# Start-up merged into the attention loop, and the feed-forward as one unrolled block with other engines for its maxima

## The reference, cut to what matters

```
h = tok(x)            # x 16x256x128: 5-step windows -> linear 640->256, +b, relu, batch norm with running mean, var
h = h + attn(layernorm(h))   # 252 rows per sequence, 16 heads of 16, bias by distance (32 buckets), causal softmax, Wo, +bo
h = h + ffn(layernorm(h))

def ffn(x):           # act_qdq: scale = max|x| over the WHOLE tensor / 32767, round, times scale
    x    = act_qdq(x)
    up   = act_qdq(x @ dq4(w_up).T)              # dq4: 4-bit weights, one scale per 32
    gate = act_qdq(x @ dq4(w_gate).T)
    gate = act_qdq(gate * round16(sigmoid(gate)))
    o    = act_qdq(gate * up)
    return o @ dq4(w_down).T
```

## Time and profile before

| what | us |
|---|---|
| three runs, median (lowest to highest) | 849.69 (849.53 to 849.99) |
| the profiled execution | 851.06 |
| its span, first to last instruction | 849.2 |
| busy: PE, DVE, ACT, POOL | 621.2, 619.2, 430.2, 182.2 |
| mean granted clock of PE, as a share of full speed | 0.893 |

### The profile page before, as it was taken

The page is one execution under the profiler, slowest core; times in us unless marked ns, Lnnn a source line. Parts: engine busy times, 40 slices in busy tenths (PEclk is TensorE's granted clock), DMA queues, the critical chain, the costliest instruction groups (busy, mean ns, idle before and its releaser), DMA issues. The chain is left out here.

```text
span 849.2 us, 15260 instructions
## 1 busy us (share of the span) xinstructions
PE 621.2 (73%) x5130; PEld 464.5 (55%) x5130; DVE 619.2 (73%) x965; ACT 430.2 (51%) x622; POOL 182.2 (21%) x228
## 2 busy tenths in 40 slices
PE   2625789898999988998989886299997720002998
PEld 1224577777777777777777654144443310002998
DVE  5656777898888888888988763346579996995442
ACT  0501434664446654466544553144498872444772
POOL 1121221122211222212222000000036552550000
PEclk9976999999999999999999975599999975555999
DMA  6233022221333312333122200000033312661343
GB/s 178 89 124 44 11 35 46 57 47 29 50 44 56 54 29 41 47 53 56 32 38 51 39 13 13 13 0 0 0 147 154 158 53 73 218 220 49 113 133 97
DMA packets 40063, 57.37 MB, mean 68 GB/s; under 512 B 5820, under 2 KB 31868, under 8 KB 40028
## 3 DMA queue, kind: packets, MB, share of 16 engines
q1 hardware_dynamic: 38876, 56.13, 26.2%
q10 hardware_dynamic: 1152, 0.79, 0.4%
HBM read 25.06 MB, written 19.13 MB: 52 GB/s over the span
## 5 line engine op out<-in xcount | busy, mean ns | idle before, releaser
L724 DVE TENSOR_REDUCE mx<-ps 126x2 f32<-126x504 f32 (+1 forms) x192 | 124.6, 674 | 44.4 <-PE ps L585 44.0
L1376 PE MATMUL ps<-wdT,oh 128*126 128x256 f16 x384 | 66.2, 280 | 92.7 <-DVE ol L1336 92.7
L807 ACT ACTIVATE pt<-sbr 126x504 f32<-126x504 f32 x192 | 114.8, 617 | 26.1 <-DVE sbr L715 24.9
L715 DVE TENSOR_TENSOR sbr<-ps,biasT 126x504 f32<-126x504 f32 x192 | 120.0, 675 | 8.9 <-PE ps L603 8.4
L1376 PEld LDWEIGHTS ps<-wdT,oh 128*126 128x126 f16 x384 | 48.9, 140 | 93.5 <-DVE ol L1336 93.5
L582 PE MATMUL ps<-biasN,identb 126*126 126x504 bf16 x192 | 75.8, 395 | 25.6 <-DMA k_st<-kl 25.6
L880 POOL TENSOR_TENSOR h<-h,bc 126x512 f32<-126x512 f32 x16 | 20.2, 1266 | 291.0 <-ACT h L821 291.0
L585 PE MATMUL ps<-k_st,q_st 65*126 65x252 f16 (+1 forms) x512 | 76.2, 252 | 0.0
L1047 PE MATMUL ps<-x2t,wgT 128*128 (+1 forms) x288 | 63.7, 386 | 11.0 <-DVE x2t L1090 11.0
L1047 PE MATMUL ps<-x2t,wuT 128*128 (+1 forms) x288 | 63.4, 376 | 11.1 <-ACT raw L1216 11.0
L585 PEld LDWEIGHTS ps<-k_st,q_st 65*126 65x126 f16 x512 | 61.5, 142 | 16.2 <-issue 1.9
(11 more groups left out here) (174 smaller groups left out, 1428.7 us busy)
## 6 DMA issues: line engine op xcount, KB each, us to landing
up_raw<-raw SPq DMA_DIRECT2D x14, 756.0 KB, 3.2
raw<-up_raw SPq DMA_DIRECT2D x14, 756.0 KB, 4.4
q_st<-qh SPq DMA_DIRECT2D x32, 128.0 KB, 4.0
k_st<-kh SPq DMA_DIRECT2D x32, 128.0 KB, 4.0
res<-hall SPq DMA_DIRECT2D x16, 252.0 KB
hin<-res SPq DMA_DIRECT2D x16, 252.0 KB
out<-y SPq DMA_DIRECT2D x16, 252.0 KB
xin<-in_x SPq DMA_DIRECT2D x16, 128.0 KB, 3.6
```

Source lines behind the costliest of these rows:

```text
L715: nc.vector.tensor_tensor(sbr[0:TT, n % 4].rearrange("p (h w) -> p h w", w=w), ps[0:TT, score_bank[name, n], 0:2 * N].rearrange("p (h w) - ...
L724: nc.vector.tensor_reduce(mx[0:TT, 0 if w == TT else 1, heads[0]:heads[-1] + 1], ps[0:TT, score_bank[name, n], 0:2 * N].rearrange("p (h w) ...
L807: nc.scalar.activation(pt[0:TT, n // 3 % 2, n % 3], sbr[0:TT, n % 4], ACT.Exp).then_inc(S["exp_r"], 1)
L1376: last = nc.tensor.matmul(ps[0:TT, s, t * C:(t + 1) * C], o[par][:, m, rows], wdT[:, w, m], start=(m == 0 and i == 0), stop=(m == MT - 1 a ...
```

## The change

The two first blocks become one and the two last become one. `sp_first`, `pool_first`, `dve_first`, `act_first`, `pe_first` run ahead of step -2 and call step -3 in their middle; the tiles of the start-up lie in buffers of the attention that are not used yet. Identity and mirror image are loaded. The running variance is loaded as a row for every partition, and POOL takes its `pow` on 128x256 numbers. `biasN` stays reversed: the mirror image takes the place of the identity in the matmul that adds it to the scores. `biasT` is put in order in step -1. Attention weights are split one after the other, the last (Wo) in step -1.

Of the feed-forward weights only the gate's is loaded and prepared in the attention (steps -1 and 0); up and down are loaded at the start of the feed-forward and prepared by DVE, PE and ACT between the gate's units. All maxima over partitions become a PE transpose of a broadcast column and a DVE maximum over 128 columns.

The feed-forward has no loops. The first two units of the up product go ahead of the last two of the gate; `raw` has five buffers; five units are never written to DRAM; ACT, not POOL, rounds the up product; the first sequence pair of the down product is made in six pieces instead of two. The last piece of the diff is ACT's loop over the gate's units, where `take` copies an up unit to `raw`.

```
-                nc.gpsimd.tensor_tensor(var[:], var[:], nhalf[:], ALU.pow).then_inc(S["vec_ready"], 1)
...
+            pool.wait_ge(S["vec_in"], 96)
+            nc.gpsimd.tensor_scalar(vec[:, 1, :], vec[:, 1, :], EPS, 1.0, ALU.add, ALU.mult
...
+            nc.gpsimd.tensor_tensor(vec[:, 1, :], vec[:, 1, :], nhalf[:, 0:1].broadcast_to([128, C]), ALU.pow
...
+            sp.dma_start(cw_n, cw.rearrange("(o p) k -> p o k", p=128)).then_inc(S["cw_in"], 16)
+            load_x(sp, 0)
...
+            sp.dma_start(biasN[0:TT], bass.AP(line_n, 0, [[1, TT], [LINE, H], [1, N]])).then_inc(S["biasN_in"], 16)
+            sp.dma_start(flipT[0:TT], bass.AP(line_t, 0, [[1, TT], [LINE, H], [1, N]])).then_inc(S["bias_in"], 16)
+            sp.dma_start(ff_view(0), ff_dram[0]).then_inc(S["ff_in0"], 16)
...
-        FF_DVE = {(-2, ("u", 2)): [("ffabs", 0)], (-2, ("stats", 2)): [("ffdq", 0, 0)],
-                  (-2, ("xnl", 2)): [("ffdq", 0, 1)], (-1, ("kl", 1)): [("ffdq", 0, 2), ("ffpow", 0)]}
+        FF_DVE = {(-2, ("u", 2)): [("wlo", 0, 1)], (-2, ("stats", 2)): [("wlo", 0, 2)], (-1, P1[2]): [("wlo", 0, 3)],
+                  (-1, ("ql", 2)): [("ffabs", 0), ("ffdq", 0, 0)], (0, P2[1]): [("ffpow", 0)]}
+        for i, at in enumerate((P1[0], P1[1], P1[2], P1[3], P1[4], P1[5], P1[6], P1[7])):
+            FF_PE[-1, at] = [("flip", 0, i)]
...
+        def over_partitions(pe, name):
+            wait(pe, "ared", SPREAD.index(name) + 1)
+            nc.tensor.transpose(spread_at(name), col[name].broadcast_to([128, 128]), identf[:]).then_inc(S["par"], 1)
+        def gathered(dve, name):
+            wait(dve, "par", SPREAD.index(name) + 1)
+            small(dve, nc.vector.tensor_reduce(col["p" + name], spread_at(name), X, ALU.max))
...
+        SEQ = [("g", t) for t in range(TL - 2)] + [("u", 0), ("g", TL - 2), ("u", 1), ("g", TL - 1)]
+        SEQ += [("u", t) for t in range(2, TL)]
...
+                def up_and_down(c):
+                    if c == 0:
+                        ff_largest(dve, 1)
+                        ff_largest(dve, 2)
+                    elif c == 1:
+                        power(dve, 6, 8, 4, 7, 256)
...
+                        ff_integers(dve, 1)
+                    elif c == 2:
+                        ff_integers(dve, 2)
+                for c in range(CH - 1):
                     integers(c + 1)
+                    largest_gate(2 * c)
+                    up_and_down(c)
+                    if 0 <= 2 * c - 5 < len(late):
+                        late_low(2 * c - 5)
+                    largest_gate(2 * c + 1)
+                    if 0 <= 2 * c - 4 < len(late):
+                        late_low(2 * c - 4)
...
+                for t in range(TL):
+                    wait(act, "p_r", t - 2)
+                    nc.scalar.activation(gq[t % 3][:], gat[:, t], ACT.Copy, scale=col["inv_g"]
...
+                    nc.scalar.activation(sig[t % 2][:], gq[t % 3][:], ACT.Sigmoid, scale=col["size_g"]
+                    if t + 3 < TL:
+                        take(t + 3)
```

More of the change, by code:

```diff
@@ new lines, in square, with spread @@
+        def square(w, part, km, i):
+            cols = w[:, part, km // 2, km % 2 * 128:km % 2 * 128 + 128]
+            return cols.rearrange("p (r s) -> p r s", s=8) if i < 2 else cols
+        def spread(pe, first, end, bank, at):
+            pe.wait_ge(S["wamax"], end)
+            for i in range(first, end):
+                last = nc.tensor.transpose(ps[:, bank, at + (i - first) * 128:at + (i - first + 1) * 128],
+                                           wam[:, i:i + 1].broadcast_to([128, 128]), identf[:])
+            last.then_inc(S["wspread"], 1)
@@ new lines, in pe_first @@
+        def pe_first(pe):
+            pe.wait_ge(S["consts"], 32)
+            for i in range(2):
+                nc.tensor.matmul(ps[0:H, i, 0:LINE], rel_s, hot_s[:, i * LINE:(i + 1) * LINE],
+                                 start=True, stop=True).then_inc(S["lines_ps"], 1)
+            pe.wait_ge(S["ident"], 16)
+            pe.wait_ge(S["cw_in"], 16)
+            for j, group in enumerate(banks):
+                for n, g in enumerate(group):
+                    last = nc.tensor.transpose(ps[:, 2 + j, n * 128:(n + 1) * 128], g[0], identf[:])
+                last.then_inc(S["wT_ps"], 1)
+            pe_step(pe, -3, 1)
+            spread(pe, 0, 1, 4, 256)
+            spread(pe, 1, 5, 5, 0)
@@ L970, in _ @@
             def _(pool):
-                for b in range(-3, 2):
+                pool_first(pool)
+                for b in range(-2, 2):
                     pool_step(pool, b, b % 2)
@@ L1059, in audio_tower @@
[L1059 to L1074 removed]
+        RING, KEPT = 5, 5
@@ L1334, in low @@
+                def low(c):
+                    for i, (m, e) in enumerate(pieces_of(c)):
+                        wait(dve, "oh_r", pieces_before(c) + i + 1)
+                        if i == 0 and c >= 2:
                             for bb in range(2):
-                                wait(dve, f"dn_ps{2 * par + bb}", k)
-                        nc.vector.tensor_tensor(flat(ol[par], hf), flat(oq, hf), flat(oh[par], hf), ALU.subtract
-                                                ).then_inc(S["ol_r"], 1)
@@ L1381, in _ @@
-                from_zero(pe, CH // 2, body)
+                over_partitions(pe, "ax")
+                for kind, t in SEQ:
+                    if kind == "g":
+                        wait(pe, "xq_r", t // 2 + 1)
+                    elif t == 0:
+                        wait(pe, "ff_lo", first_late + len(late))
+                    banks_free(pe, kind, t)
+                    product(kind, t).then_inc(S["g_ps" if kind == "g" else "u_ps"], 1)
+                    if (kind, t) == ("g", 2):
+                        spread(pe, 6, 8, 7, 256)
+                    elif kind == "g" and 5 <= t < 5 + len(late):
+                        j = t - 5
+                        wait(pe, "wdq_w", 2 + j // (len(late) // 2))
+                        wait(pe, "wall", 4)
+                        wait(pe, "ff_lo", first_late + j - 1)
+                        for n, g in enumerate(late[j]):
+                            last = nc.tensor.transpose(turned(j)[:, n * 128:(n + 1) * 128], g[0], identf[:])
+                        last.then_inc(S["ffT_ps"], 1)
+                    elif (kind, t) == ("u", 2):
+                        over_partitions(pe, "ag")
```

1049 lines of the change are left out of this document (534 added, 515 removed).

## The result

| kernel | runs | median us | lowest to highest |
|---|---|---|---|
| before, beside it | 20 | 851.63 | 847.13 to 856.42 |
| changed | 20 | 854.08 | 852.41 to 855.91 |

The ratio is 1.0034, with a 95% interval of 1.0021 to 1.0047: the changed kernel is slower by a third of a per cent. Its profiled execution took 854.10 (span 852.3). The forecast was 824, the range ended at 846, and slower had 12 chances in 100. The case that came is a rival of the prediction, the wide `pow`.

The account below looks back on a forecast made before the run. No engine was taken as the limit throughout: start-up chains and idle joints could gain, added DVE or PE work lose. Terms -23.7 - 5.3 + 16 - 12.8 = -25.8 took 851.06 to 825.3, forecast 824 against the median, range 815 to 846.

Parts of the forecast that it names:

- the wide `pow`: Start-up rival: POOL multiplies nothing before its 128x256 `pow` ends; chance 0.18 for 15 to 38 us, 0.12 above (slower kernel).
- the first term: Start-up and the way to the first `P1`: -32 us, with a `pow` of up to 12 us hidden.
- The rest of the start-up term: The -32 us apart from the `pow`: second x lands at 34, first normalised transpose at 34.7, then 15.0 to `P1`.
- Steps -1 and 0: Attention steps: +8.5 us, of it +1 mirror-image products, +6 DVE's work on the gate's weight, +1.5 inside step 0.
- Maximum of x: Joint at x's maximum: -5.3 us, with PE transpose, DVE maximum and hand-overs, 0.9, in place of 6.2 of waiting.
- Gate product: Gate's start to first sigmoid product: +16 us, 92 in place of 76.0, with 7.8 of PE pauses.
- the rival at 814 to 819: Late weights weigh less: DVE works ahead in the gate's window and the 7.8 us of pauses go; chance 0.1.
- Up stage: Up stage: -1.7 us, from two maxima taken earlier (-3.4), steps inside (+0.9) and a slip in the second unit (+0.8).
- Joint ahead of o, o stage, down: From the up stage's end on: joint ahead of the first o product -6.4 us, o stage -4, down -0.7.
- The swap that gains nothing: Rival at the joints, by the skill's rule: moving reductions from POOL to PE and DVE gains nothing, 836 us; chance 0.04.

Follow-up runs that it names:

- pow128: Changed kernel with the `pow` taken of 128 of the 256 columns: 833.61 us, ratio 0.9782 to the kernel before.
- pow64: Changed kernel with the `pow` taken of 64 of the 256 columns: 823.92 us, ratio 0.9677 to the kernel before.
- narrow: Changed kernel with the running variance again as 128x2 numbers for POOL's `pow`, made a row through DRAM: 815.24 us, ratio 0.9582 to the kernel before.
- n_step: `narrow` with DVE preparing one block of 32 of the 48 of the gate's weight: 809.96 us, ratio 0.9506 to the kernel before.
- n_pool: `narrow` with the maxima of x and o over the partitions taken by POOL's reduction again: 822.29 us, ratio 0.9658 to the kernel before.
- n_ahead: `narrow` with DVE rounding x for the gate two pairs of sequences ahead in place of one: 814.64 us, ratio 0.9568 to the kernel before.
- n_plain: `narrow` with all 16 gate units ahead of the first up unit, one up maximum ahead in place of three: 811.58 us, ratio 0.9526 to the kernel before.
- narrow_end: `narrow` with its two-column tile declared last, so `q_st` and `k_st` lie as in the changed kernel: 825.82 us, ratio 0.9702 to the kernel before.
- before_pad: Kernel before with an unused two-column tile behind `nhalf`, moving `q_st` and `k_st` to multiples of 64 bytes: 841.81 us, ratio 0.9869 to the kernel before.

## Why the prediction was wrong

**The step that failed** is a choice of size in the first term: "I take the geometric middle, 10 us, which is still covered". The `pow` takes 41.15, between the ends of 1.3 and 71. The mechanism behind it ("each us above 12 is a us of time") is right: what the `pow` lost in `pow128`, the kernel lost too. The 12 is too much, since 9.3 are covered (`pow64`). That 825.3 + (41.15 - 12) = 854.45 comes so near to the 854.10 of the profiled execution is therefore in part luck: the cover was 2.7 smaller than assumed, and the other terms came out 2.2 lower than forecast. The forecast rested on a mean between a row of equal width and a row of equal operation. The nearer row was the one of equal operation: what the 128x2 `pow` paid above the addition, 0.55 for two columns, is 0.275 a column, and the true price is 0.159 with some 0.3 once. Half a microsecond on two columns was the evidence for the slow case, and I gave that case, above the 38 us where it decides, 12 in 100.

**The rest of the start-up term** is right within some 1, as `narrow` shows: `P1` at 50.8 in place of 49.7, with the second x as the last to come, some 1.5 later than I had it.

**Steps -1 and 0** (+8.5): 9.1. The +6 for DVE's work on the gate's weight is what `n_step` takes away, 5.3. The "2.04 at the slow clock" for a mirror-image product is read from its length alone: the granted clock of that stretch is 1.00, though the next products of this shape take 1.01 at 37.84.

**Maximum of x** (-5.3): -5.2. The reading that POOL is late at this joint, and that a change on POOL makes it late, is borne out by `n_pool` and by the pairs of `MODIFY_POOL_CONFIG`. It doesn't hold for every joint: where the change falls into idle time, as at o, POOL is as quick as PE.

**Gate product** (+16): +15.4, and the sum hides a size: the pauses came where I put them, 1.2, 3.4 and 0.2 in place of 1.3, 4.0 and 2.5, so 4.7 and not 7.8. That the sum came out right all the same is in part luck: the clock fell behind the longest pause and made one unit 1.7 longer (5.67 against 3.99), which is no term of the prediction. The busy time of the 288 matmuls with the gate's weight, 67.1 in place of 63.7 before, can't be put down to the clock as a whole: the product now comes in many pieces, and a unit that stands alone counts 3.99, while units that follow each other start 3.83 apart (617.68 and 621.51). That the pauses could be worked away for a gain (the rival at 814 to 819) isn't borne out by `n_ahead`, one way to try it. The price of the two up units in front is shown by `n_plain`: 8.5 in the gate, 2.9 given back.

**Up stage** (-1.7): -4.9. The two up maxima taken earlier are right: one stood ahead of the first sigmoid product before (617.52), three do now. The steps inside are there as well, 0.8 (711.17 to 711.93). What the term leaves out is the length of a unit, 5.15 from product to product before (L1127 at 634.52 and 639.67) and 4.92 now (L1275 at 648.03 and 652.95). Before, the maximum that reads a product starts 1.88 behind it (634.52 to 636.40), and the other operations start 1.64 apart. Now an up maximum stands between, and all start 1.64 apart; where none is left, it is 1.77 (711.93 to 713.70). That this order is the cause is read from the rows; no run changes it alone. **Joint ahead of o, o stage, down**: within 0.5 each.

**The swap that gains nothing** (the rule, 836): at x it is worth 8 us, at o nothing. The joints of the gate and of the up product, where the change back to ordinary work took 6.9 and 6.7 before, are not put back in any run. What stays of the change without the wide `pow` is a gain of 3.0% (`narrow_end`); with it the change loses 0.3%.

## What to carry to other kernels

Before an operation is widened, get its price for each column from two widths, or by its excess over a plain operation at the width that is there; a mean between far ends isn't evidence. A row that is alike in all partitions is cheaper as a few columns spread over them. A wait that is moved ahead of everything on an engine has to be covered in full: here some 9 us were covered and 32 were not. A POOL reduction that follows ordinary work cost 8 us here where POOL had to change at the joint itself, and nothing where it had idled ahead of it. When a kernel's steady loop changes speed and no instruction in it did, compare the addresses of the tiles that its transfers touch.

## What the runs showed of the hardware that was not expected

- GpSimd's `pow` in f32: 0.159 us a column and some 0.3 once, the same for 16 partitions (41.13 for 256 columns) as for 128 (41.15).
- Tiles moved by 32 bytes change this kernel by 1%: 128 KB from tile to tile in 3.8 in place of 4.2 us, 0.5 us in every step, and a gain of 1.3% for the kernel before by one unused tile (`before_pad`).
- POOL's change between ordinary instructions and a reduction over partitions takes 5.7 to 8.7 us from `MODIFY_POOL_CONFIG` to the next instruction, and each change pays it, in both directions (kernel before, `n_pool`). On the spot it keeps DVE waiting 9.22 us at x; at o, with the change hidden in idle time, DVE waits 0.59. The reduction itself is 0.41 in both.
- A pause of PE of 3.4 us inside a dense product was followed by a unit that took 5.67 in place of 3.99.
